# A three-branch layer on one core: another prologue, and an output projection from high and low parts

## The reference

```python
x = x + attn_a(layernorm(x), Wqkv, bqkv, Wo, bo)      # 16 heads of 32, masked softmax, then out @ Wo + bo
x = x + ffn(layernorm(x), Wr, br, Wd, bd, Wu, bu)     # 8 experts of rank 16, the best 2 by a softmax gate
x = x + attn_b(layernorm(x), W_in, conv_w, conv_b, z_bias, D, W_out)
    # proj = u @ W_in.T; a 4-tap causal convolution over xBC; y from decayed C.B products
    # (32 heads, state 64, head size 16); y * silu(z) @ W_out.T
x = x + ffn(layernorm(x), ...)                        # the same weights again
```

## Time and profile before

| | |
|---|---|
| median of 3 runs | 3271.09 us (3270.25 to 3282.86) |
| the profiled execution | 3254.58 us, its span 3253.0 us |
| mean granted clock of TensorE | 0.962 of full |
| TensorE busy | 3014.0 us, 93% |
| VectorE, ScalarE, GpSimd busy | 68%, 34%, 23% |
| bytes moved by DMA | 191.57 MB |

### The profile page before, as it was taken

One profiled execution on the slowest core, in us unless ns is written; L12 is line 12 of the kernel. 1 busy time (PEld: TensorE's weight loads), 2 busy tenths in 40 slices (PEclk: granted clock), 3 DMA queues, 4 the chain that ended last, 5 costly groups with the idle time before them and its releaser, 6 DMA issues.

```text
span 3253.0 us, 59676 instructions
## 1 busy us (share of the span) xinstructions
PE 3014.0 (93%) x20772; PEld 2069.4 (64%) x20772; DVE 2205.5 (68%) x2975; ACT 1096.9 (34%) x1733; POOL 761.4 (23%) x1071
## 2 busy tenths in 40 slices
PE   3589999999999998999989999999999999999998
PEld 3445457777755446777765444777776454677776
DVE  1356667777656667777775666777766566687777
ACT  1223414444213333343412332443431333244342
POOL 3121111333221111233312110133330211123332
PEclk7799999999989999999999999999999999999999
DMA  7422102111231211111122220111112311021112
GB/s 232 157 51 66 46 14 65 49 46 36 67 86 46 65 27 46 51 45 50 50 75 60 51 65 20 53 45 51 45 44 86 72 45 46 14 73 46 50 45 75
DMA packets 161189, 191.57 MB, mean 59 GB/s; under 512 B 43962, under 2 KB 103994, under 8 KB 159226
## 3 DMA queue, kind: packets, MB, share of 16 engines
q1 hardware_dynamic: 157150, 175.83, 19.5%
q0 software_dynamic: 2720, 10.49, 0.8%
q10 hardware_dynamic: 1152, 3.15, 0.5%
HBM read 106.99 MB, written 23.36 MB: 40 GB/s over the span
## 4 chain that ended last, share of the span: by engine, by line
PE 75%; DVE 11%; issue 4%; DMA 4%; SPq 3%; ACT 2%; POOL 1%; ACTq 0%; DVEq 0%; POOLq 0%
PE ps L723 13%; PE ps L725 12%; PE ps L724 12%; PE ps L875 7%; PE ps L838 5%; PE ps L858 5%; PE ps L1056 4%; PE ps L942 3%; PE ps L1042 2%; PE ps L1102 2%; DVE LM L1660 2%; PE ps L1065 2%; DMA KS<-EV 1%; DVE mneg L1567 1%; PE ps L733 1%
## 5 line engine op out<-in xcount | busy, mean ns | idle before, releaser
L723 PE MATMUL ps<-uh,win 128*128 128x512 f32 x1536 | 630.8, 411 | 4.9 <-POOL win L1820 4.3
L725 PE MATMUL ps<-uh,win 128*128 128x512 f32 x1536 | 605.3, 394 | 0.0
L724 PE MATMUL ps<-ul,win 128*128 128x512 f32 x1536 | 602.4, 392 | 0.0
L1567 DVE TENSOR_REDUCE mneg<-ps 128x1 f32<-128x128 f32 (+7 forms) x512 | 362.0, 752 | 146.1 <-PE ps L841 142.9
L1239 ACT ACTIVATE PR<-ps 128x1024 f32<-128x1024 f32 (+3 forms) x384 | 310.5, 810 | 406.6 <-PE ps L861 270.0
L723 PEld LDWEIGHTS ps<-uh,win 128*128 128x128 f32 x1536 | 290.9, 189 | 96.6 <-issue 29.6
L875 PE MATMUL ps<-PR,VG 128*32 128x512 f32 (+3 forms) x1536 | 336.3, 514 | 12.5 <-DVE OS L1573 8.3
L877 PE MATMUL ps<-PR,ones 128*32 128x512 f32 (+3 forms) x1536 | 336.3, 514 | 0.0
L1684 DVE TENSOR_TENSOR LM<-ps,LM 128x512 f32<-128x512 f32 x256 | 170.1, 686 | 243.2 <-PE ps L1056 197.2
L725 PEld LDWEIGHTS ps<-uh,win 128*128 128x128 f32 x1536 | 290.3, 189 | 66.0
L724 PEld LDWEIGHTS ps<-ul,win 128*128 128x128 f32 x1536 | 291.5, 190 | 54.9
(11 more groups left out here) (220 smaller groups left out, 5140.7 us busy)
## 6 DMA issues: line engine op xcount, KB each, us to landing
raw<-in_t SPq DMA_DIRECT2D x128, 256.0 KB, 2.7
QS<-EV SPq DMA_DIRECT2D x192, 128.0 KB, 2.4
KS<-EV SPq DMA_DIRECT2D x168, 128.0 KB, 2.4
X<-in_L_attn_b_W_in_dram SPq DMA_DIRECT2D x10, 1024.0 KB, 7.8
in_t<-tiles POOLq DMA_DIRECT2D x10, 1024.0 KB, 8.4
XN<-in_L_attn_a_x_dram SPq DMA_DIRECT2D x40, 256.0 KB, 4.7
win_raw<-in_L_attn_a_Wqkv_dram SPq DMA_DIRECT2D x34, 256.0 KB, 3.3
win_raw<-in_t SPq DMA_DIRECT2D x32, 256.0 KB, 2.7
```

Source lines behind the costliest of these rows:

```text
L723: pe.matmul(dst, hi_l, hi_r, start=first, stop=False)
L724: pe.matmul(dst, hi_l, lo_r, start=False, stop=False)
L725: return pe.matmul(dst, lo_l, hi_r, start=False, stop=last)
L1567: dve.tensor_reduce(mneg[:, hh, t:t + 1], wide(b0)[:, 0:(t + 1) * P], AX.X, ALU.max, negate=True).then_inc(a_max.sem, 1)
```

## The change

The prologue gets four row buffers (the two halves of X and two more over tiles not yet in use), and its loops are written out. The two constants for the transpose (`ident`) are made first, with a semaphore of their own. SyncE issues four row loads, then Wv and the first Wq, Wk slices, the tokens of batch 0, and the small loads between the further row loads; the loads of `conv` and `dsk` come last, on `s_late`, for which engines wait behind the attention. ScalarE, not GpSimd, issues the stores to `in_t`. `first_barrier` is gone; in its place stand single waits. VectorE takes the statistics of batch 0's first seven token tiles before the small subtractions. The eight semaphores for token tiles become one, and the first wait of a batch is for all eight. Last, the attention's output projection is made from parts: `wo` is split in the last group, OT piece by piece, and 128 fp32 products become 384 in F32R.

```diff
+ROW_BUFS = 4
+ROW_TILES = 10
...
+            more_rows = sb("more_rows", [P, 2, KT, D], at=c2)
...
-        s_x = [sem(f"s_x{t}") for t in range(TT)]
+        s_x = sem("s_x")
...
-        def first_barrier(eng):
-            eng.drain().then_inc(s_bar, 1)
-            eng.wait_ge(s_bar, 5)
-            eng.sem_inc(s_tick, 1)
...
-            rows = X[:, :, :].rearrange("p (a k) d -> p a k d", a=2)
+            rows = [X[:, i * KT:(i + 1) * KT, :] for i in range(2)] + [more_rows[:, i] for i in range(2)]
...
+                woh_a = sb("woh_a", [P, KT, D], F32R, at=c2)
+                wol_a = sb("wol_a", [P, KT, D], F32R, at=c2)
...
+                OTl = sb("OTl", [P, GROUPS, L], F32R, at=c2)
...
+                OTh = sb("OTh", [P, GROUPS, L], F32R, at=c2)
...
-        LOADS = 50
+        LOADS = 16
+        LATE = 34
...
-            def load_rows(n, par):
-                sp.dma_start(rows[:, par, :, :], W_in[bass.ds(n * D, D), :].rearrange("(r p) d -> p r d", p=P)
-                             ).then_inc(s_pre_in[par], 16)
-            for par in range(2):
-                load_rows(par, par)
+            def load_rows(n):
+                src = W_in[n * D:(n + 1) * D, :] if n < ROW_TILES else W_out
+                if n >= ROW_BUFS:
+                    sp.wait_ge(s_pre_pe, (n - ROW_BUFS + 1) * KT)
+                sp.dma_start(rows[n % ROW_BUFS], src.rearrange("(r p) d -> p r d", p=P)).then_inc(s_pre_in[n % ROW_BUFS], 16)
+            def group_weights(g):
+                for w in range(2):
+                    sp.dma_start(win_raw[:, 0, w, 1],
+                                 Wqkv[:, bass.ds(g * P + w * D, P)].rearrange("(k p) n -> p k n", p=P)).then_inc(s_qkw, 16)
+            def value_weights():
+                sp.dma_start(wv_raw[:, 1], Wqkv[:, 2 * D:3 * D].rearrange("(k p) n -> p k n", p=P)).then_inc(s_wv, 16)
+            def load_tokens(b):
+                for t in range(TT):
+                    sp.dma_start(XN[:, t, :], x[bass.ds(b, 1), t * P:(t + 1) * P, :].rearrange("a p d -> p (a d)")).then_inc(s_x, 16)
+            for n in range(ROW_BUFS):
+                load_rows(n)
+            value_weights()
+            group_weights(0)
             load(bqk[:, :], bqkv[0:2 * D].rearrange("(t p) -> p t", p=P))
+            load_rows(4)
+            load_tokens(0)
+            load_rows(5)
             load(bvb[:, :], bqkv[2 * D:3 * D].partition_broadcast(P))
             load(bob[:, :], bo.partition_broadcast(P))
+            load_rows(6)
             load(bz[:, 0:ER], bd.rearrange("e r -> (e r)").partition_broadcast(P))
             load(bz[:, ER:ZC], br.partition_broadcast(P))
-            load(conv[:, :, 0:TAPS], conv_w.rearrange("(t p) o c -> p t (o c)", p=P))
-            load(conv[:, :, TAPS:TAPS + 1], conv_b.rearrange("(t p o) -> p t o", p=P, o=1))
             load(zb[:, :], z_bias.rearrange("(t p) -> p t", p=P))
-            for m in range(KT):
-                for h in range(P // HD):
-                    load(dsk[h * HD:(h + 1) * HD, m:m + 1],
-                         Dskip[m * 8 + h:m * 8 + h + 1].partition_broadcast(HD))
+            load_rows(7)
             for k in range(KT):
                 load(wdf[:, k, 0:ER].rearrange("p (e r) -> p e r", r=R),
                      Wd[:, k * P:(k + 1) * P, :].rearrange("e p r -> p e r"))
             load(wdf[:, :, ER:ZC], Wr.rearrange("(k p) e -> p k e", p=P))
+            load_rows(8)
             load(wu[:, :], Wu.rearrange("e r d -> (e r) d"))
             for i in range(3):
                 load(buf[i * E:(i + 1) * E, :], bu)
+            load_rows(9)
             load(arow[:, :], W_in[A_ROW:A_ROW + NH, :])
-            with sp.Fori(0, 4) as i:
-                for par in range(2):
-                    sp.wait_ge(s_pre_pe, (i * 2 + par + 2) * KT + 1)
-                    load_rows(i * 2 + par + 2, par)
...
-            sp.wait_ge(s_pre_pe, 10 * KT + 1)
-            sp.dma_start(rows[:, 0, :, :], W_out.rearrange("(r p) d -> p r d", p=P)).then_inc(s_pre_in[0], 16)
+            load_rows(10)
+            load(conv[:, :, 0:TAPS], conv_w.rearrange("(t p) o c -> p t (o c)", p=P), s_late)
+            load(conv[:, :, TAPS:TAPS + 1], conv_b.rearrange("(t p o) -> p t o", p=P, o=1), s_late)
             sp.wait_ge(s_pre_bul, 1)
             sp.dma_start(bu3[2 * E:3 * E, :].bitcast(F32), bul[2 * E:3 * E, :].bitcast(F32)).then_inc(s_pre_st, 16)
+            sp.wait_ge(s_grid_pool, 6)
...
+            for m in range(KT):
+                for h in range(P // HD):
+                    load(dsk[h * HD:(h + 1) * HD, m:m + 1],
+                         Dskip[m * 8 + h:m * 8 + h + 1].partition_broadcast(HD), s_late)
             sp.wait_ge(s_pre_st, 16 * 3)
...
-            pe.sem_inc(s_pre_pe, KT + 1)
-            pe.wait_ge(s_const, 2)
-            with pe.Fori(0, 5) as i:
-                for par in range(2):
-                    n = i * 2 + par
-                    pe.wait_ge(s_pre_in[par], i * 16 + 16)
-                    pe.wait_ge(s_pre_ca, n * 2 + 1)
-                    pe.wait_ge(s_pre_cd, n * 2 + 1)
-                    for r in range(KT):
-                        for k in range(KT):
-                            t = pe.transpose(ps[:, par * KT + r, k * P:(k + 1) * P],
-                                             rows[:, par, r, k * P:(k + 1) * P], ident[:, :])
-                        t.then_inc(s_pre_pe, 1)
-            pe.wait_ge(s_pre_in[0], 16 * 6)
-            pe.wait_ge(s_pre_ca, 10 * 2 + 3)
-            pe.wait_ge(s_pre_cd, 10 * 2 + 3)
+            pe.wait_ge(s_ident, 2)
+            for n in range(ROW_TILES):
+                pe.wait_ge(s_pre_in[n % ROW_BUFS], (n // ROW_BUFS + 1) * 16)
+                if n >= 2:
+                    pe.wait_ge(s_pre_ca, (n - 1) * 2)
+                    pe.wait_ge(s_pre_cd, (n - 1) * 2)
+                for r in range(KT):
+                    for k in range(KT):
+                        t = pe.transpose(ps[:, n % 2 * KT + r, k * P:(k + 1) * P],
+                                         rows[n % ROW_BUFS][:, r, k * P:(k + 1) * P], ident[:, :])
+                    t.then_inc(s_pre_pe, 1)
...
-            first_barrier(pe)
+            pe.wait_ge(s_const, 1)
+            pe.wait_ge(s_pre_act, KT)
+            pe.wait_ge(s_pre_low, 3)
...
-                pe.wait_ge(s_wo, b * 16 + 16)
+                wo_lo.wait(pe, b, 1)
                 row_product(lambda dst, k, t0, first, end:
-                            pe.matmul(dst, OT[:, k, t0:t0 + P], wo[:, k, :], start=first, stop=end),
-                            b * 2, lambda: o_scaled.wait(pe, b * 8 + 5, 2), lambda: o_scaled.wait(pe, b * 8 + 7, 2))
+                            three(dst, OTh[:, k, t0:t0 + P], OTl[:, k, t0:t0 + P], woh_a[:, k, :], wol_a[:, k, :], first, end),
+                            b * 2, lambda: ot_lo.wait(pe, b, 2 * GROUPS - 2), lambda: ot_lo.wait(pe, b, 2 * GROUPS))
+                pe.wait_ge(s_pre_st, 16 * 3)
...
-            act.sem_inc(s_pre_ca, 3)
-            with act.Fori(0, 5) as i:
-                for par in range(2):
-                    n = i * 2 + par
-                    act.wait_ge(s_pre_out[par], i * 16)
-                    for r in range(2):
-                        act.wait_ge(s_pre_pe, n * KT + (KT + 1 + r + 1))
-                        act.copy(tiles[:, par, r, :], ps[:, par * KT + r, :]).then_inc(s_pre_ca, 1)
+            for n in range(ROW_TILES):
+                par = n % 2
+                if n >= 2:
+                    act.wait_ge(s_pre_out[par], n // 2 * 16)
+                for r in range(2):
+                    act.wait_ge(s_pre_pe, n * KT + r + 1)
+                    act.copy(tiles[:, par, r, :], ps[:, par * KT + r, :]).then_inc(s_pre_ca, 1)
+                act.wait_ge(s_pre_ca, (n + 1) * 2)
+                act.wait_ge(s_pre_cd, (n + 1) * 2)
+                act.dma_start(in_dram[n * KT:(n + 1) * KT].rearrange("t p f -> p t f"), tiles[:, par]).then_inc(s_pre_out[par], 16)
...
+                def output_hi(k, c):
+                    cols = slice(c * HB, (c + 1) * HB)
+                    o_scaled.wait(act, b * 8 + 2 * k + 1, c + 1)
+                    act.copy(OTh[:, k, cols], OT[:, k, cols]).then_inc(ot_hi.sem, 1)
...
+                                if hf == 0 and last and u == 1:
+                                    act.wait_ge(s_wo, b * 16 + 16)
+                                    vg_done.wait(act, p + 1, 1)
+                                    act.copy(woh_a[:, :, :], wo[:, :, :]).then_inc(wo_hi.sem, 1)
+                                if hf == 1 and last and u >= 4 and u < 4 + 2 * (GROUPS - 1):
+                                    output_hi((u - 4) // 2, u % 2)
                                 if hf == 0 and not last and u - 1 in PROJECT_AT:
                                     project_hi(g + 1, PROJECT_AT.index(u - 1), False)
+                for c in range(2):
+                    output_hi(GROUPS - 1, c)
                 experts(b * 4 + 1, b * 2)
+                act.wait_ge(s_late, 16 * LATE)
```

(87 more changed lines are left out.)

73 lines of the change are left out of this document (36 added, 37 removed).

## The result

| | before | after |
|---|---|---|
| median of the runs | 3269.1 us (3259.3 to 3285.0) | 3248.4 us (3239.3 to 3281.6) |
| ratio, 95% interval | | 0.9947, 0.9925 to 0.9969 |
| profiled execution, span | 3254.6, 3253.0 us | 3261.0, 3259.3 us |
| first product, `values(0)` | 125.3 us | 87.4 us |
| output projection of the attention, four batches | 110.9 us | 88.3 us |

By the medians of twelve runs each the kernel became 20.7 us faster (10 to 25 by the interval), where 55 were forecast. Both big terms came as forecast (-37.9 and -22.6 us), and some 40 us came back between them. So spans are not compared, but stages that agree in all four batches.

What follows compares the result with a forecast made beforehand. TensorE's own work and its standstills, chiefly before the first product, were taken to bound the kernel. Prologue -38, output projection -21, split work +4 gave -55 us: 3271 to 3216 us, range 3200 to 3240.

Steps and rivals of the forecast that it cites:

- (a), (b): Prologue: 24.8 MB at 380 GB/s take 65.3 us, small packets 4 us more; tile 9 copied at about 74 us.
- (c): Prologue: store pairs through ScalarE's queue take 10.4 us each, four end at 52 to 62 us; bytes bound it, not buffers.
- (d): Prologue after tile 9: statistics and small subtractions take about 13 us, GpSimd's subtractions are covered; `values(0)` starts at 87 us.
- (e): Barrier's removal: SyncE is busy through the dsk loads to about 101 us, first stacking of Q at 113, 12 us of cover.
- Output projection, price of a product: Attention's output projection: fp32r products 0.233 us apart, 22.4 us a batch, saving 5.3 us a batch, 21 us in four.
- Output projection, first half: Last group's first half: weight cast and subtraction mostly fit idle gaps, 1 us a batch sticks out; bounds nothing to 16.7 us.
- rival 2: Output projection: the split is not hidden, casts delay exponentials, 16.7 + 13 instead of 4 us; 3242 us, chance 0.06.
- Second half and tail: Last group's second half and behind: 0.55 us casts fit ScalarE's gaps, cost nothing, bound 13 us; tail covered by 1.5 us.
- Rival 1: Prologue: the stores pace it, `values(0)` starts at 104 us; 3233 us, chance 0.10.
- 4: Rival, prologue: ScalarE's store queue is served late, landings take over 30 us, kernel slower; 3299 us, chance 0.02.
- rival 3: Prologue and projection: DMA engines keep 397 GB/s and nothing of the split sticks out; 3204 us, chance 0.10.
- rival 5: Whole kernel: no effect, bytes bound the prologue as before and the split costs what it saves; chance 0.02.

Runs made afterwards that it cites:

- experiment 7: Experiment 1's kernel with the 32 dsk loads back ahead of the fifth row load and none behind the rows: 3220.1 us, ratio 0.9835.
- Experiment 2: Changed kernel with the weight cast at its place but writing its own tile, the wait for VG moved to VectorE ahead of the subtraction: 3201.9 us, ratio 0.9799.
- experiment 4: Kernel before, plus only ScalarE's wait for the VG copy behind the last group's second exponential: 3301.1 us, ratio 1.0114.
- experiment 1: Also called cast_later: changed kernel with the weight cast behind four more exponentials and its subtraction in the second half: 3207.3 us, ratio 0.9827.
- experiment 9: Experiment 1's kernel with four semaphores for the token tiles, one for each pair, instead of one: 3207.5 us, ratio 0.9827.
- experiment 11: Kernel before, plus one unread 0.87 us product in front of the scores that wait for stacked Q and K: 3243.2 us, ratio 0.9928.

## Why the prediction was off

- **Mechanism of the gain: right.** Two standstills and one expensive stage were to shrink, and did: 38 us forecast and 37.9 found, 21 and 22.6.
- **Prologue (a), (b): right.** Tile 9 copied at 73.0 us for 74 forecast; the DMA engines full from 10 us. Their rate was lower than assumed (364 for 380 GB/s, which makes 2.8 us more of the same bytes), so that the end came out within 1 us on terms that partly cancel is in part luck. That dsk's place mattered is shown (experiment 7); the 4 us for the other small packets was only an estimate.
- **(c): right, with one weak reason.** The `in_t` stores land in 5.1, 8.2 and 12.4 us (shortest, median, longest), forecast 8.4 and 4.9 to 11.0. "Bytes bound it, not buffers" is true of four buffers alone: two make it 2 to 6 us later. ScalarE's longest wait for a landing was 7.8 us.
- **(d): right.** `values(0)` at 87.4 us for 87; GpSimd's four subtractions end at 83.0, covered as forecast.
- **(e): right.** The dsk loads stand in SyncE's queue from 85.4 to 105.5 us, some four us later than put down, and the first stacking of Q is issued at 112.1 us, for 113 forecast.
- **Output projection, price of a product: right to 3%,** 0.2267 us for 0.233.
- **Output projection, first half: this is the step that failed.** The prediction said that the cast falls between the second and third exponential, where ScalarE is idle 1.61 us, and that 0.3 to 0.5 us stick out. It priced the cast by its duration and the gap around it. It did not count the wait that stands ahead of the cast in the diff, though the diff brought it and `woh_a` lies over V. In the trace of before, ScalarE's second exponential of that half ends at 369.2 us and GpSimd's copy of V at 374.8:

```profile
368.78 0.38 ACT L1239 ACTIVATE PR<-ps 128x256 f32<-128x256 f32 x1 [0.49 <-PE ps L861]
```

```profile
374.15 0.62 POOL L1845 COPY VG<-V 128x512 f32 x1 [0.25 <-POOL OT L1875]
```

These rows were in reach, and would have given 5.6 us a batch for the stall alone. The true price is 10 us a batch, not 1. Experiment 2 shows that the step as it was reasoned is right for a cast without the wait, experiment 4 what the wait alone takes, and experiment 1 that behind four more exponentials the cast is free.

- **The bound of that step was no bound.** "All of it, 16.7 us" counted the work added. Neither the waiting time (22.5 us) nor the clock was in it, so the range ended at 3240, and even rival 2 at 3242 had the wrong mechanism.
- **The clock.** The prediction looked for a clock that stays low only behind the first product. By what it asked of ScalarE's stores in (d) (what is queued behind one, and who waits for that) it could have followed the stall of 5.6 us on ScalarE to TensorE's standstill, 5.4 us. That the clock would fall with it, for 4.5 us more, stood in no row of the attention that it shows.
- **Second half and tail: right.** The last group's second half takes 20.2 us in both kernels, and TensorE has no stall in the new projection. The terms were small but misread: ScalarE's idle time there is not 0.64 us at least, the trace of before has 0.49 and 0.50 us too, and the casts take 0.61 us and the subtractions 0.83, for 0.55 and 0.57. That it cost nothing even so was not worked out. **Tokens counted together: right** (experiment 9).
- **Rivals.** None was it. Rival 1 (stores pace the prologue) and 4 fall with `values(0)` at 87.4; rival 3 did not come in the prologue; rival 5 falls with the two stages.

## What to carry to other kernels

Price an added instruction by its waits first and by its duration second: look up when the last thing that it waits for ends in the trace of before, above all where its target lies over a buffer that is still read, and put it behind that moment. Where TensorE has to stand still for microseconds in a dense stretch, look at the granted clock behind the hole. In this kernel moving the wait elsewhere was best (41 us), and products that nobody reads gave back more than they cost (23 us). Compare stages that repeat in all batches rather than two profiled spans when runs differ by more than the effect.

## What the runs showed of the hardware

**The clock behind a hole of TensorE.** With 5.4 us of standstill the granted clock fell in every batch (35.2 us at a mean of 0.81, that is part of the half at 1.2 GHz and the rest at 2.4), and 4.5 us of the 10 were its doing. With 3.7 us of it (experiment 4) the half took 33.8 us in every batch, at a mean of 0.80. The page TensorE: Matmul & The Clock Gate of the Trainium skill (section HAM oscillation — how this bites in real kernels) says that long idle gaps behind waits put the clock down, so that the next tile starts cold. For this hole the trace agrees.

**Short holes too, and not always.** Behind a hole of 1.3 us, with TensorE busy some 95% of the half, a half took 26.3, 29.3 or 36.3 us, the last at a clock of 0.67. It differs from batch to batch and from one execution to the next of the same kernel. One unread product of 0.87 us in the hole ended it in all of the twelve halves of both profiled kernels that have it, and was worth 29 us in one (3207.3 to 3178.3) and 26 in the other (3269 to 3243). It is probably also the reason for much of the spread between runs: the changed kernel's executions at 3239.3 and 3281.6 us had mean granted clocks of 0.958 and 0.944, and six runs of cast_later lie 22 us apart, six with the product 7. What decides whether a given short hole brings the fall stays open. A hole of TensorE of 3.0 to 3.5 us ahead of the second group's projection, where it waits for GpSimd's subtraction of W_in, is in some batches of both kernels and was left unfilled. In experiment 11 the half with that wait takes 40.9 us in batch 1, and 44.0 in batch 2, without the wait and at a clock of 0.77. What this hole costs stays open.

**The order of small loads.** 32 loads of a few bytes hold SyncE's queue for 17.5 us before, 20.1 after and 20.7 in experiment 7; there, ahead of the row loads, they cost 8 to 12 us of the start. Beside the first products no later work was seen to wait for them: the queue is free at 105.5 us, and the first stacking, at 112.1, waited for VectorE. **Stores in ScalarE's queue** landed as fast beside SyncE's deep one (8.2 us median) as they had in GpSimd's (8.4).
